# A two-layer transformer kernel: tiles of the experts listed in two parts, output biases added at the tiles, results four deep, and the first maxima of layer 1 in plain slot order

## The reference, cut to what matters

```python
xn = layernorm(x)
x = x + attention0(xn) + fp4_ffn(xn)        # 16 heads of 8 channels; gate, up, down 128 x 352,
                                            # values and weights rounded to FP4 in blocks of 16
xn = layernorm(x)
x = x + attention1(xn) + moe(xn)            # biases on q, k, v and out

def moe(x):                                 # 8 experts, hidden 512, the best 2 of each token
    logits = relu(x @ Wr1 + br1) @ Wr2 + br2
    tg, ti = top_k(softmax(logits), 2); tg = softmax(tg / 2)
    out = silu(x @ Ws1 + bs1) @ Ws2 + bs2
    for e in range(8):
        out += sum(tg * (ti == e))[:, None] * (silu(x @ We1[e] + be1[e]) @ We2[e] + be2[e])
    return out
```

## Time and profile before

| | us |
|---|---|
| median of three runs (1424.39 to 1443.83) | 1429.02 |
| the profiled execution | 1434.63 |
| its span, first to last instruction | 1432.9 |
| PE busy | 1155.4 (81%) |
| DVE busy | 934.5 (65%) |
| ACT busy | 797.5 (56%) |
| POOL busy | 459.0 (32%) |

### The profile page before, as it was taken

One profiled execution on the slowest core, in us unless ns is written; L12 is line 12 of the kernel. 1 busy time (PEld: TensorE's weight loads), 2 busy tenths in 40 slices (PEclk: granted clock), 3 DMA queues, 4 the chain that ended last, 5 costly groups with the idle time before them and its releaser, 6 DMA issues.

```text
span 1432.9 us, 19562 instructions
## 1 busy us (share of the span) xinstructions
PE 1155.4 (81%) x6807; PEld 520.0 (36%) x6807; DVE 934.5 (65%) x1600; ACT 797.5 (56%) x1077; POOL 459.0 (32%) x409
## 2 busy tenths in 40 slices
PE   2679667988898888888888988898889737888994
PEld 1212313422342343234323432243233125787841
DVE  6857747778777877877787768777872435532323
ACT  1344446476766667675767476657576402233373
POOL 9541352135224332223323333321421201344420
PEclk9667789999999999999999999899999759999997
DMA  5512073107411731261146204610510372456644
GB/s 154 117 61 57 11 198 115 34 1 193 129 34 37 189 97 34 84 189 49 35 118 172 58 9 133 174 36 7 152 34 1 95 185 85 142 174 183 182 139 124
DMA packets 149508, 144.13 MB, mean 101 GB/s; under 512 B 13689, under 2 KB 141890, under 8 KB 149410
## 3 DMA queue, kind: packets, MB, share of 16 engines
q1 hardware_dynamic: 143922, 132.96, 34.5%
q0 software_dynamic: 4544, 9.38, 2.0%
q10 hardware_dynamic: 944, 0.54, 0.1%
HBM read 90.19 MB, written 52.12 MB: 99 GB/s over the span
## 4 chain that ended last, share of the span: by engine, by line
PE 38%; DVE 16%; ACT 15%; DMA 9%; issue 7%; DVEq 6%; SPq 4%; POOL 3%; ACTq 0%; POOLq 0%
DVE nm L1054 8%; PE sums L387 8%; PE mx L399 7%; ACT ex L768 6%; PE mx L368 4%; ACT L746 4%; PE mx L489 3%; PE mx L498 3%; DMA ks<-xsort 2%; PE ring L473 2%; PE ring L289 2%; DMA scratch<-parts 2%; PE ring L299 2%; PE ring L294 2%; PE ring L356 1%
## 5 line engine op out<-in xcount | busy, mean ns | idle before, releaser
L768 ACT ACTIVATE ex<-mx 128x1024 f32<-128x1024 f32 x512 | 511.9, 1023 | 332.2 <-PE mx L399 331.6
L1054 DVE TENSOR_REDUCE nm<-mx 128x2 f32<-128x1024 f32 x512 | 600.6, 1216 | 133.9 <-PE mx L368 133.2
L399 PE MATMUL mx<-qs,ks 128*128 128x512 bf16 (+1 forms) x1024 | 312.9, 401 | 53.4 <-ACT hs L759 13.3
L387 PE MATMUL sums<-ex,vs 128*18 128x512 f32 x2048 | 297.3, 636 | 3.2 <-ACT ex L768 1.3
L399 PEld LDWEIGHTS mx<-qs,ks 128*128 128x128 bf16 (+1 forms) x1024 | 77.1, 99 | 341.9 <-issue 144.0
L368 PE MATMUL mx<-km,qm 32*128 32x512 bf16 x1024 | 149.6, 410 | 63.7 <-DVE nm L1054 38.1
L368 PEld LDWEIGHTS mx<-km,qm 32*128 32x128 bf16 x1024 | 37.9, 92 | 218.8 <-issue 84.4
L1470 POOL TENSOR_SCALAR binade<-binade 128x704 f32<-128x704 f32 (+1 forms) x24 | 56.3, 2347 | 188.7 <-DVE binade L1005 188.7
L1495 POOL DMA_INDIRECT xsort<-xn,pos_i x64 | 62.6, 978 | 169.0 <-DVE pos_i L1141 151.7
L1462 POOL TENSOR_TENSOR parts<-qk_f,parts 128x512 bf16<-128x512 f32 x32 | 36.9, 1174 | 181.7 <-DVE parts L973 181.7
L1433 POOL TENSOR_TENSOR rstd<-veps,minus_half 128x4 f32<-128x4 f32 x16 | 16.7, 1045 | 210.0 <-DVE veps L964 210.0
(11 more groups left out here) (212 smaller groups left out, 1568.3 us busy)
## 6 DMA issues: line engine op xcount, KB each, us to landing
scratch<-parts SPq DMA_DIRECT2D x128, 256.0 KB, 3.6
ks<-scratch SPq DMA_DIRECT2D x64, 256.0 KB
qs<-scratch SPq DMA_DIRECT2D x64, 256.0 KB
qs<-wmoe SPq DMA_DIRECT2D x20, 514.0 KB, 3.6
ks<-wmoe SPq DMA_DIRECT2D x19, 514.0 KB, 3.7
qm<-scratch SPq DMA_DIRECT2D x64, 128.0 KB, 2.6
km<-scratch SPq DMA_DIRECT2D x64, 128.0 KB, 2.6
rest<-parts SPq DMA_DIRECT2D x32, 128.0 KB, 3.3
```

Source lines behind the costliest of these rows:

```text
L387: done = pe.matmul(acc[32 * j:32 * j + 2 * VW, :], values[:, start:start + 2 * VW], ex[:, s % NEX, j, :], start=q == 0 and t == 0, stop=q ...
L399: done = pe.matmul(bank[:, j, :], ks[l][r, h, t * P:(t + 1) * P], qs[l][r, h, :], start=True, stop=True)
L768: act.activation(ex[:, s % NEX, 2 * i:2 * i + 2, :], bank[:, :, :], ACT.Exp, scale=SCALE).then_inc(free, 1)
L1054: dve.tensor_reduce(nm[l][:, t, h:h + 2], bank[:, :, :], AX.X, ALU.max, negate=True).then_inc(free, 1)
```

## The change

- `NFULL` = 21 tiles are sure to be full of tokens of batches 0 to 6. DVE lists them at the start of `turn_b(7)` (`tile_table(0)`), SP fetches tiles 0 and 1 there, and the tile steps begin with slot 0 of `turn_a(8)` (`FIRST_TILE` is 0). The other 18 are listed behind the last router (`tile_table(1)`); the clears stand ahead of the fetch of tile 4, the second half of the last stacks ahead of tile 8, stores and rows ahead of tiles 12 and 21. The weights of tile i now wait until DVE has read the result of tile i - 4.
- The biases of the experts are 128 more columns of the fetched weights (`WROW` 1156 instead of 1028) and are added by DVE as it reads a tile's result. `gates_transposed`, the nine-row products and the gate tables go. The shared bias is added to the output bias of the attention once, on POOL.
- Results and bases have four buffers each (`NRES`).
- `turn_a(1)` has one unit in each slot. Twelve units instead of ten stand ahead of `turn_a(0)`, and batch 1's units begin in its slot 6. `max_rows` moves from slot 1 to the end of slot 0, and the steps of `quantize_h` later, with their waits for POOL only where data would be overwritten. POOL rounds h ahead of `third_part(1, b)`. The table loads around the first gates go.

The core of the diff; the moved places in `work_a` and `work_b` are cut to DVE's:

```diff
-FIRST_TILE = 6
-FIRST_UNITS = 10
-FIRST_SHIFT = 3
+FIRST_TILE = 0
+FIRST_UNITS, FIRST_NEXT = 12, 6
 NTILE = 2 * B * T // TS + E - 1
-WROW = FE + EC * P + EC
-NW = 4
+NFULL = -(-(2 * (B - 1) * T - E * (TS - 1)) // TS)
+WROW = FE + EC * P + EC + P
+NW, NRES = 4, 4
...
-            if b == 1:
-                first, last = FIRST_SHIFT, SLOTS - FIRST_SHIFT
-                return [(1, 0, u) for u in ([k - first] if first <= k < last else [2 * k - SLOTS, 2 * k - SLOTS + 1] if k >= last else [])]
             if b >= 1:
                 return [(1, b - 1, k)]
             if k < SLOTS - FIRST_UNITS:
                 return [(0, 0, FIRST_UNITS + k)]
-            return [(0, 1, k - 8)] if k >= 8 else []
+            return [(0, 1, k - FIRST_NEXT)] if k >= FIRST_NEXT else []
 
         def units_b(b, k):
             if b == 0:
-                return [(0, 1, 8 + k)] if k < 8 else []
+                return [(0, 1, SLOTS - FIRST_NEXT + k)] if k < FIRST_NEXT else []
             return [(0, b + 1, k)] if b < LAST else []
...
             def gates(b, i):
-                load_table(ACT.Silu, 8 * b + 2 * i)
+                if b >= 1:
+                    load_table(ACT.Silu, 8 * b + 2 * i)
                 bank, free = from_pair(("gate", b, i))
                 act.activation(h_sb[:, 2 * i:2 * i + 2, :], bank[:, :, 0:F0], ACT.Silu).then_inc(free, 1)
-                load_table(ACT.Exp, 8 * b + 2 * i + 1)
+                if b >= 1:
+                    load_table(ACT.Exp, 8 * b + 2 * i + 1)
...
 
-            def gates_transposed(b):
-                pe.wait_ge(w9_ready, b + 1)
-                transpose_tiles(("wT", b), lambda t: w9[:, t, :], cols=E + 1)
-
             def shared_out(b):
-                ring_read(pe, ("wT", b))
                 pair_read(pe, ("H", b, 1))
                 bank = to_ring(("o", b))
                 for t in range(NT):
                     for c in range(EC):
-                        pe.matmul(bank[:, t * P:(t + 1) * P], hs[:, c, t * P:(t + 1) * P], w2_sb[:, c, :], start=c == 0, stop=False)
-                    done = pe.matmul(bank[:, t * P:(t + 1) * P], w9T[:, t * P:(t + 1) * P], b2_sb[:, :], start=False, stop=True)
+                        done = pe.matmul(bank[:, t * P:(t + 1) * P], hs[:, c, t * P:(t + 1) * P], w2_sb[:, c, :],
+                                         start=c == 0, stop=c == EC - 1)
                 done.then_inc(ring_full, 1)
...
             def quantize_h(b, i, step):
                 if step == 0:
-                    wait(dve, xq_ready, b + 1)
-                    wait(dve, h_ready, 2 * b + i)
                     dve.drain()
                     quantize_maxima(h, 2 * F0)
                 if step == 1:
+                    wait(dve, xq_ready, b + 1)
                     quantize_scales(2 * F0, qsc[i])
                 if step == 2:
                     quantize_scaled(h, h, 2 * F0)
                 if step == 3:
+                    wait(dve, h_ready, 2 * b + i)
                     quantize_binades(h, 2 * F0, binade[:, :]).then_inc(h_scaled, 1)
...
-            def tile_table():
+            def tile_table(part):
+
+
+                columns = slice(0, NFULL) if part == 0 else slice(NFULL, NTILE)
+                n = columns.stop - columns.start
+                number = iota_t[:, 0:n]
+                behind, steps = after[:, 0:n, :], used[:, 0:n, :]
+                expert, row = t_exp[:, columns], t_row[:, columns]
 
...
+                if part == 0:
+                    p, before = pairs.at(("E", 0, LAST, SLOTS - 1, 1))
+                    dve.wait_ge(mx_full[p], before + 1)
+                dve.drain()
+                if part == 1:
+                    dve.memset(zeros, 0.0)
+                    dve.tensor_copy(end_row[:, :], count[:, :]).then_inc(ends_ready, 1)
                 dve.tensor_tensor(n_exp[:, :], count[:, :], ebase[:, :], ALU.subtract)
                 dve.drain()
-                dve.tensor_scalar(tiles_i[:, :], n_exp[:, :], float(TS - 1), None, ALU.add)
+                dve.tensor_scalar(tiles_i[:, :], n_exp[:, :], float(part * (TS - 1)), None, ALU.add)
                 dve.drain()
                 dve.tensor_scalar(tiles_i[:, :], tiles_i[:, :], 8, None, ALU.logical_shift_right)
                 dve.drain()
                 dve.tensor_copy(tiles[:, :], tiles_i[:, :])
                 dve.drain()
+                if part == 1:
+                    dve.tensor_tensor(tiles[:, :], tiles[:, :], taken[:, :], ALU.subtract)
+                    dve.drain()
                 dve.tensor_tensor_scan(ends[:, :], one8[:, :], tiles[:, :], 0.0, ALU.mult, ALU.add)
                 dve.drain()
...
+                dve.tensor_tensor(behind, number.unsqueeze(2).broadcast_to([P, n, E]), over(ends), ALU.is_ge)
+                if part == 0:
+                    dve.tensor_tensor(begins[:, :], ends[:, :], tiles[:, :], ALU.subtract)
+                    dve.memset(skip[:, :], 0.0)
+                    dve.drain()
+                    dve.tensor_scalar(begins[:, :], begins[:, :], -1.0, float(NFULL), ALU.mult, ALU.add)
+                    dve.drain()
+                    dve.tensor_scalar(begins[:, :], begins[:, :], 0.0, None, ALU.max)
+                    dve.drain()
+                    dve.tensor_tensor(taken[:, :], begins[:, :], tiles[:, :], ALU.min)
+                    dve.drain()
+                    dve.tensor_tensor(skip[:, 0:E - 1], taken[:, 1:E], taken[:, 0:E - 1], ALU.subtract)
+                dve.drain()
+                if part == 1:
+                    dve.tensor_tensor(tiles[:, :], tiles[:, :], skip[:, :], ALU.subtract)
+                    dve.drain()
+                dve.tensor_reduce(expert, behind, AX.X, ALU.add)
+                dve.tensor_tensor(steps, behind, over(tiles), ALU.mult)
+                dve.drain()
...
+                if part == 1:
+                    dve.tensor_scalar(row, row, taken[:, 0:1], None, ALU.add)
+                    dve.drain()
...
+                dve.tensor_scalar(x_row[:, columns], row, count[:, E - 1:E], None, ALU.min).then_inc(tiles_ready, 1)
 
...
             def tile_out(i):
                 bank, free = from_pair(("TO", i))
                 wait(dve, y_out[i % 2], i // 2 * 32)
-                dve.tensor_copy(yo[i % 2], bank[:, 0, 0:TS]).then_inc(free, 1)
+                bias = wbuf[i % NW][:, WROW - P:WROW]
+                dve.tensor_tensor(yo[i % 2].rearrange("p (h c) -> p h c", c=P), bank[:, 0, 0:TS].rearrange("p (h c) -> p h c", c=P),
+                                  bias.unsqueeze(1).broadcast_to([P, 2, P]), ALU.add).then_inc(free, 1)
...
-                    if at == (1 if b else 6, "a"):
+                    if at == ((0, "d") if b else (SLOTS - FIRST_UNITS, "a")):
                         max_rows(0, b, 1)
-                    if at == (0, "c"):
+                    if at == (1, "m"):
                         quantize_h(b, 1, 0)
-                    if at == (1, "m"):
+                    if at == (2, "m"):
                         quantize_h(b, 1, 1)
-                    if at == (2, "m"):
+                    if at == (2, "c"):
                         quantize_h(b, 1, 2)
-                    if at == (2, "c"):
+                    if at == (5, "m"):
                         quantize_h(b, 1, 3)
                     if at == (14, "a"):
                         ffn_down(b)
...
+                    if at == (0, "a"):
+                        tile_table(0)
                     if at == (11, "b"):
                         places(b)
-                        tile_table()
                     if at == (12, "a"):
                         router_weights(b)
+                        tile_table(1)
...
             def fetch_weights(i):
                 first = sp.value_load(w_row[0:1, i:i + 1], min_val=0, max_val=(E - 1) * P)
                 if i >= NW:
-                    p, before = pairs.at(("TO", i - NW))
-                    sp.wait_ge(mx_full[p], before + 1)
+                    pair_read(sp, ("TO", i - NW))
                 sp.dma_start(wbuf[i % NW], wmoe[bass.ds(first, P), :]).then_inc(w_in[i % NW], 16)
...
+            def load_results(b):
+                wait(sp, summed, b - NRES + 1)
+                for c in range(2):
+                    first = c * PLANE + 1 + b * T
+                    sp.dma_start(yb[b % NRES][:, c, :, :], y2[first:first + T, :].rearrange("(t p) c -> p t c", p=P)).then_inc(yb_in[b % NRES], 16)
+
+            def load_base(b):
+                wait(sp, result_out[b % NRES], 16 * (b // NRES))
+                sp.wait_ge(base_out, 16 * (b + 1))
+                sp.dma_start(fb[b % NRES], base[b].rearrange("(t p) c -> p t c", p=P)).then_inc(fb_in[b % NRES], 16)
+
...
                 if b + 1 <= LAST:
                     load_rows(0, b + 1, 0)
+                if b == LAST:
+                    sp.wait_ge(tiles_ready, 1)
+                    fetch_weights(0)
+                    sp.wait_ge(scattered, 16 * 8 * LAST)
+                    fetch_tokens(0)
```

(43 more changed lines are left out.)

152 lines of the change are left out of this document (60 added, 92 removed).

## The result

The changed kernel takes **1358.55 us** (median of 4 runs, 1354.87 to 1365.04) against 1432.11 (4 runs, 1424.39 to 1443.83): ratio 0.9485, 95% interval 0.9407 to 0.9562. That is 73.6 us where I had forecast 51.6; the time lies inside my range, near its lower end and almost on rival C's 1357. The profiled execution took 1365.04 us (span 1363.3), the longest of its four and 69.6 under the one before. Of the runs of the kernel before that stood beside the experiments, three of 1445 to 1452 us at a lower granted clock are left out of the comparisons.

What follows compares the result with a forecast made beforehand. No engine bounds the whole; PE leads in the turns, waits dominate around the experts. Terms 8 + 8.4 + 15.8 + 1 + 0.7 - 1.3 + 14 + 5 = 51.6 off 1434.6 give 1383, median 1380 us; forecast 1368 to 1390, wider range 1356 to 1408.

Steps and rivals of the forecast that it cites:

- rival C: Whole kernel: turns a lose most extra in slots 1 to 3, tiles keep 4.3 us; 72 us gain, 1357 us; chance 0.13.
- the plain order: Turn a(1): one layer-1 unit per slot from slot 0 replaces three double final slots, which cost 4.7 us more.
- Output biases: Last slot of layer-0 turns: removing four bias pairs saves 1.64 us per batch; gate transposes elsewhere save 0.5 us.
- turns a(2) to a(7): Layer-0 turns of batches 2 to 7: 6 x (1.64 + 0.5 + 0.5) = 15.8 us gained.
- Row step in turns b: Slot 1 of six turns b: moving the row step to slot 0's end saves 1.4 us each, 8.4 us.
- Rivals B: Turns keep their length as waits move to pair banks or ACT; 27 us gain, 1402 us; chance 0.20.
- Turn a(1): Batch 1's layer-0 turn: plain unit order, earlier row step and bias removal gain 8 us, bounds 0 and 12.
- Rival E: Turn a(1): plain order only moves the wait to slot 0; already counted in the 8 us; no chance given.
- Start and turn a(0): Before turn a(0): four table loads go, row step comes earlier, two units added; 1 us gain, bounds -2 and 6.
- The expert part: Tiles: steps beside the last maxima, then 4.6 us per tile instead of 4.3; 14 us gain, bounds -10 and 33.8.
- Rival D: Tiles: each waits for its own tokens, 6.9 us per tile; 30 us slower overall, 1459 us; chance 0.03.
- Results: Kernel's end: four-deep results remove DVE's waits for loads; 5 us gain, at most 5.1.

Runs made afterwards that it cites:

- The experiment: Kernel before without the nine-row bias products, the gates' transposes, ACT's copy and DVE's three small products for them: 1407.32 us, ratio 0.9812.
- 4 by the experiment: Changed kernel with results two deep again and the old order of loads and stores at the end: 1362.58 us, ratio 0.9502.
- one swapped line: Changed kernel with one line of SP's loop moved, so a tile's tokens are fetched ahead of its weights: 1331.90 us, ratio 0.9293.

## Why the prediction was right, and where its sizes were off

**Right: direction, range and the waits that I had named.** The time is outside 1368 to 1390, to which I gave 0.44, and its nearness to rival C's 1357 is luck: C let the tiles keep 4.3 us, and they took 4.7. (C and the other rivals were reckoned from 1429.0, my forecast from 1434.6 less 3; on its footing C stands at 1360.) In most parts the mechanism holds and the size was off, mostly to the low side. It was wrong in turn a(1), where the plain order costs, in the start, where two of the four table loads stayed, and in turns a, where the moved wait gave nothing by itself.

**Output biases.** The mis-sized term: 1.64 per batch was 2.33, and 0.5 was 0.7. I measured the pair by the gap to the next round and took the round beside it as fixed. The experiment gave 24.2 us for this part where my steps have 2.14 x 7 = 15. A third of the missing 15 us in turns a(2) to a(7) is here: (2.33 + 0.7 - 2.14) x 6 = 5.3. Another 4 are in slots 9 to 11 of turn a(6), 14.3 us before and 10.3 after; the clock had fallen there for 13.7 us before, behind no wait that the change moved, and it did not fall after.

**Row step in turns b.** 1.4 each was the wait; the slot gained it and slot 0 gave 0.5 back (3.1 to 3.6), as I had reckoned only for turns a. An undisturbed turn b gained 0.8 (62.9 to 62.1), less than the 1 us that I had asked of it. The total of 10.6 is above my 8.4 because turns b(1) and b(5), 66.5 and 66.2 us before, each had a fall of the clock of 6.8 us at slot 1, and none there after.

**What no step had: the clock.** I read the wait rows and priced the wait alone. In the trace before, the clock was 0.5 behind the ring wait of slot 1 at 472.0 and 608.5, and such a slot was 6.7 us long against 5.3 in turns a without it. Rivals B and C did not name it either. From 228 to 1050 us there are 37.5 us less at 0.50 after; at the 1.4 us that slot 1 lost with each fall of 3.4, I estimate 15 us of the gain from these figures, a part of which is in the row step's 20. The Trainium skill ("TensorE: Matmul & The Clock Gate", HAM oscillation) warns of a fall at each DMA wait, and I applied that to the tiles only. Turn a(8) after, PEclk in the stretches:
```profile
1082.60:1102.20 19.60, 5.81 (x20) 3.31 (x21) 6.51 (x14) 2.04 (x5) 2.20 (x3) 0.50 0.84 234
...
1105.60:1115.70 10.10, 6.87 (x53) 5.75 (x51) 6.39 (x11) 3.13 (x8) 3.83 (x4) 1.00 0.60 183
1115.70:1119.10 3.40, 3.40 (x9) 2.80 (x10) 0.94 (x5) 0.00 (x0) 0.00 (x0) 0.51 0.46 159
```
The fall behind the wait of 3.23 is there, as that rule has it, but the clock had also come back between the waits, which I had left out.

**Turn a(1).** 8 forecast, 9.2 measured, for the wrong reason: my 4.7 for the double slots and 3.0 for the start were real parts, but the run with the old unit order is 4.7 us shorter in this turn. In that run the turn lost 13.9 us (87.2 to 73.3): about 4 with the bias products (4.1 in the kernel without them), the other 10 with the quantising behind the row step and POOL's order; the plain order, which I took for the cause, costs. Rival E, that the wait only moves to slot 0, is what happened to this piece.

**Start and turn a(0).** I wrote off the start as 1 us and gave nothing back for the two units moved ahead. They cost 4.6 us before the turn and saved 5.5 in it. The total of the two stretches is 5.8, of which 1 was forecast. ACT's loads were not hidden behind DVE, and of the four I had removed two came back.

**The expert part.** 14 forecast, 8.8 measured between first maxima and last exponentials. The pace was nearly right (4.72 for 4.6); the slots were not: 16 of them took 116 us from 1082.56, and I had walked 107, with slots 7 and 8 at 8.6 and 7.8 where they took 8.9 and 10.8. The rest of the loop came out at 110 for my 112. Turn b(7) up to the first maxima gave 1.1 where I had lost 0.6. Rival D's 6.9 us per tile did not come. The steps beside the last maxima, the main move in this part, have no run of their own.

**Results.** 5 forecast, 3.1 by the traces, 4 by the experiment. Behind the end of the last exponential the time fell from 25.1 us to 20.2, which is my 5; the exponentials of that turn took 1.8 longer, nearly all of it in slot 2 (2.0 to 3.6), with the clock at 0.50 for 6.8 us there and 3.4 before. I had depth as the only limit; the loads of base rows 4 to 6, placed behind every store, held DVE:
```profile
1337.35 2.35 DVE L1230 SCALAR_TENSOR_TENSOR qs<-qs,tg 128x128 f32<-128x128 f32 x8 [8.55 <-DMA qs<-base]
```
DVE's last combine ended behind PE's first transposes, contrary to what I said would be seen.

**The sum against the experiments:** biases 24, row step 20, plain order -3, waiting for DVE's read -5.5, results 4, the start's two parts 5 to 6 by trace: some 45. The remaining 28 or so (steps beside the last maxima, the quantising put later, the moved parts of k and v, POOL's order) were not tried alone, and their cause is open.

## What to carry to other kernels

Price a short matmul with a narrow stationary operand by the time of the block with and without it, not by its own row. Price a wait with the granted clock of the microseconds behind it. Where one engine's queue serves two streams, look for the stream whose issue must wait for a reader, and put it behind the one that need not: one swapped line gave 26.7 us here, more than any single part of the change that was tried, by the medians.

## What was not expected of the hardware

- Eight 128-row products took 0.89 us in a block of 32 and 1.09 behind a pair with nine rows.
- With the same code ahead of it, the stretch from the last slot of turn a(0) to the end of turn b(0) took 41.0 to 41.2 us in six kernels and 43.8 in seven. In each of the seven the granted clock falls to 0.50 once more, for 6.8 us, 37 us into the stretch, and in none of the six; why it falls there in some was not found.
- In ACT, taking out the explicit table loads around the first gates left two of the four in other places, one of them directly ahead of the first exponential.
